# Causal mask folded into VectorE's maximum, and a new order of a pair's units, in a fused convolution, attention and spectral kernel

## The chip, the cores and the metric

One core of a Trainium2 chip runs the whole program. The metric is the device time of one execution in microseconds (us), as the median of several runs. TensorE, VectorE, ScalarE and GpSimd are called PE, DVE, ACT and POOL in the profile; SP issues most of the DMAs.

## The reference

Input `x` is 8 images of 64 channels, 32x32 pixels, float32. Three blocks follow each other, each with a residual:

```python
x = x + _L0_conv_ref(_gn(x), offset_w, offset_b, weight, bias)   # deformable 3x3 convolution
t = _to_tokens(x)                                                 # 8 x 1024 tokens x 64
t = t + _L1_attn_ref(_ln_t(t), w_q, w_k, w_v, w_o)                # 16 heads of 64, RoPE, causal
t = t + _L1_ffn_ref(_ln_t(t), sigma, phi, M_u, M_phi_plus, M_phi_minus, log_weights, gumbel)
```

What the attention computes for each image and head is

```python
att = jnp.einsum('bqhd,bkhd->bhqk', q, k) / jnp.sqrt(E)
att = jnp.where(causal, att, -jnp.inf)
att = jax.nn.softmax(att, axis=-1)
y = jnp.einsum('bhqk,bkhd->bqhd', att, v)
```

with 1024 queries and keys. The group norm `_gn` has 32 groups of two channels.

## The kernel before

The program has three stages, one after the other.

**Front.** SP loads the inputs in the order of its program. DVE takes the moments of all four pairs of images (`bn_stats`, L364), PE averages them over the channels of a group with two small matmuls (L553, L555), ACT takes the root, and DVE writes the normalised images with a border (`pad`, L390). For each pair of images PE computes the offset convolution (`conv`, L496, 9 taps x 2 halves) and then transposes the pixels (`pixels`, L509); ACT copies them out (L587), and SP writes them as a table to HBM, 16 DMAs per pair of images (`table`, L249 and L252). DVE turns the offsets into indices and weights (`draw`, L396 on). When the table of images 0 and 1 has landed and its indices are drawn, POOL gathers for the first 10 tiles of 128 tokens (L332, 9 indirect DMAs each); each tile is weighted by DVE, multiplied on PE, added to the residual and layer-normed.

**Attention.** 64 pairs of heads (8 images x 8 pairs; `NPAIR`, `NIT`). The body of the loop holds two pairs, and every engine runs the same table `SEQUENCE` of units for a pair, in order, each taking the units that are its own. The units are:

- `("rope", r)`: PE projects queries or keys of the next pair into PSUM (cost of 1024 columns), DVE multiplies by cosine and sine (L1158, L1159), POOL adds the two (`add`, L1243).
- `("upper", r)`: ACT rounds the rotated half to fp32r for the maxima (L1101).
- `("max", x)`: PE computes scores of the next pair, queries on the partitions, for the key blocks that `MAX_OF[x]` names; DVE takes the maximum over the free axis (L1149) into `mx` or `mx_half`. The causal mask of a diagonal block (key block = query block) is added on PE: four bf16 matmuls of 128 columns into the same PSUM (L920, out of `mask_b`).
- `("merge",)`: DVE merges the halves; `("row",)`: PE transposes the maxima (L964), ACT copies them negated (L1095), SP spreads them with two DMAs into `rows_m` (L865).
- `("S", u)`: PE computes the scores again, keys on the partitions, minus the maxima from `rows_m`; ACT takes the exponential (L1083). `S 0` waits for the two DMAs of `row`. POOL zeroes the diagonal blocks (`mask` in `POOL_ORDER`).
- `("value", u, lag)`: PE multiplies the probabilities by the tokens into `psY` (L1022). It needs no slot (below). With lag 1 it belongs to the pair before.
- `("leave",)`: ACT takes `psY` out (L1075). `("out", q)`: PE projects it (L1002), DVE divides by the row sums (L1128, L1131), POOL adds it to the tokens (`token`).
- `("weigh", x)`, `("fold", a)`, `("dT",)`, `("dR",)`, `("norm",)`, `("dX",)`: one tile of the deformable convolution of the next image, gathered by POOL, weighted by DVE (L1174), folded (POOL L1273, DVE L1183), multiplied on PE (L977, L984), normed by DVE (17 small dependent instructions, L1192 to L1204) and transposed by PE (L989).

The units of PE that DVE or ACT reads go round over three slots of PSUM (`SLOTS = 3`). PE may start such a unit only when the reader of the unit three places earlier is done:

```python
by = BY_ACT if UNITS[n - SLOTS][0] in BY_ACT else BY_DVE
```

So the order of the table sets how far PE can run ahead of DVE. `AHEAD` is the list for the first pair, run once ahead of the loop.

**Spectral.** Filters over the tokens of all images. The change doesn't touch it.

## Time and profile before

| | |
|---|---|
| median of 3 runs | 2934.59 us (2934.13 to 2935.37) |
| the profiled execution, its own time | 2933.56 us |
| its span | 2931.8 us |
| front, to its last copy of tokens on DVE | 0 to 199 us |
| attention, to its last projection on PE | 202 to 2260 us |
| spectral | 2268 us to the end |
| busy: PE, DVE, ACT, POOL | 94%, 75%, 45%, 59% |

The profile is of one execution. A row of the timeline gives the start, the busy time, the engine, the line of the kernel, the operation, the tile written and the tiles read. The busy time of a merged row covers several instructions, and neighbouring instructions of an engine overlap; so where it matters how long an engine is held, the text takes the distance from one start to the next.

### The profile page before, as it was taken

Reading aid. Unit: us, or ns where it says so; the run is one execution under the profiler, and the core shown is the slowest. Engines: PE = TensorE matmul, PEld = TensorE weight load, DVE = VectorE, ACT = ScalarE, POOL = GpSimd, SP = SyncE. Lnnn points to the kernel's source line nnn. Section 1 sums busy time; section 2 is a strip of 40 time slices with the busy share of each in tenths; the row PEclk is TensorE's granted clock in tenths of the full one; section 3 lists DMA queues with packets and bytes.
Section 4 is the critical chain, followed back from the end, with each engine's and each line's share of the span. In section 5 each row is a group of like instructions: output and inputs, shape, how many; then the busy total and the mean of one; then the engine's idle time right before and its main releaser. Section 6 shows DMA issues by size and latency. Waiting matters only on the chain. (4 is left out here: it accounts for less than half of the span.)

```text
span 2931.8 us, 60696 instructions
## 1 busy us (share of the span) xinstructions
PE 2741.8 (94%) x18761; PEld 1789.2 (61%) x18761; DVE 2185.6 (75%) x3909; ACT 1330.1 (45%) x1788; POOL 1740.8 (59%) x1831
## 2 busy tenths in 40 slices
PE   3639999999999999999999999999998899999998
PEld 1335655655655655656655655655655788888887
DVE  3448788788788788788888888888886675767676
ACT  1103444444444444444444444444443465656565
POOL 3746777777777777777777777777776670000000
PEclk8659999999999999999999999999999899999999
DMA  5542222222222222222222212244443553444343
GB/s 151 145 112 59 64 63 62 64 63 58 68 63 58 68 63 58 64 67 58 65 67 58 65 54 69 65 64 60 64 65 55 161 168 116 147 130 146 116 154 105
DMA packets 159644, 249.21 MB, mean 85 GB/s; under 512 B 71662, under 2 KB 93502, under 8 KB 159582
## 3 DMA queue, kind: packets, MB, share of 16 engines
q1 hardware_dynamic: 125902, 155.61, 18.8%
q0 software_dynamic: 33680, 92.71, 13.1%
q8 instruction: 46, 0.75, 0.1%
q14 instruction: 16, 0.13, 0.0%
HBM read 230.65 MB, written 17.04 MB: 84 GB/s over the span
## 5 line engine op out<-in xcount | busy, mean ns | idle before, releaser
L1083 ACT ACTIVATE attention_probs<-attention_pss 128x1024 f32<-128x1024 f32 x576 | 590.1, 1024 | 310.7 <-PE attention_pss L920 298.4
L1286 POOL DMA_INDIRECT attention_gat<-table,attention_idx x585 | 558.5, 955 | 200.0 <-issue 121.3
L920 PE MATMUL attention_pss<-attention_kq 64*128 64x512 f32 (+3 forms) x3072 | 651.8, 483 | 0.0
L1149 DVE TENSOR_REDUCE attention_mx_half<-attention_pss 128x2 f32<-128x1024 f32 (+3 forms) x520 | 513.2, 1020 | 98.5 <-PE attention_pss L920 98.5
L1022 PE MATMUL attention_psY<-attention_probs,attention_xt 128*64 128x512 f32 (+3 forms) x3120 | 574.1, 496 | 0.2 <-issue 0.2
L1642 DVE SCALAR_TENSOR_TENSOR spectral_eo<-spectral_psE,kept_sig,spectral_eo 64x512 fp32r<-64x512 f32 x512 | 384.0, 750 | 170.1 <-ACT spectral_eo L1617 163.9
L1243 POOL TENSOR_TENSOR attention_kq<-attention_tA,attention_tB 128x512 f32<-128x512 f32 x260 | 416.1, 1611 | 111.0 <-DVE attention_tB L1159 101.7
L1535 PE MATMUL spectral_psE<-spectral_tz,spectral_up 128*128 128x512 f32 (+1 forms) x2304 | 462.1, 358 | 5.8 <-DVE spectral_up L1633 5.8
L1617 ACT ACTIVATE spectral_eo<-spectral_psE,kept_sig 64x512 fp32r<-64x512 f32 x512 | 350.2, 684 | 243.9 <-PE spectral_psE L1535 238.9
L920 PE MATMUL attention_pss<-attention_rows_m,attention_ones 64*128 64x512 f32 (+2 forms) x1536 | 458.8, 530 | 0.0
L1535 PEld LDWEIGHTS spectral_psE<-spectral_tz,spectral_up 128*128 128x128 f32 x2304 | 386.5, 189 | 78.2 <-issue 6.2
L920 PE MATMUL attention_pss<-attention_nat_h 64*128 64x512 f32 (+2 forms) x1560 | 401.8, 524 | 3.1 <-DVE attention_mx_half L1149 1.9
L920 PEld LDWEIGHTS attention_pss<-attention_kq 64*128 64x128 f32 x3072 | 316.5, 186 | 48.2 <-issue 15.3
L1022 PEld LDWEIGHTS attention_psY<-attention_probs,attention_xt 128*64 128x64 f32 x3120 | 186.4, 136 | 238.4 <-issue 208.6
L1101 ACT ACTIVATE attention_nat_h<-attention_kq 128x512 fp32r<-128x512 f32 x260 | 163.9, 630 | 331.5 <-POOL attention_kq L1243 331.5
L1158 DVE TENSOR_TENSOR attention_tA<-attention_pss,attention_cosT 128x512 f32<-128x512 f32 x260 | 178.3, 686 | 164.2 <-PE attention_pss L920 163.9
L920 PE MATMUL attention_pss<-attention_xb,attention_wt 64*128 64x512 f32 x1040 | 254.9, 610 | 17.1 <-DVE attention_xT L1142 15.2
L920 PEld LDWEIGHTS attention_pss<-attention_nat_h 64*128 64x128 f32 x1560 | 168.0, 186 | 154.9 <-issue 67.4
L920 PEld LDWEIGHTS attention_pss<-attention_rows_m,attention_ones 64*128 64x128 f32 x1536 | 199.5, 186 | 95.8 <-issue 78.2
L1174 DVE TENSOR_TENSOR attention_gat<-attention_gat,conv_Wc 128x768 f32<-128x768 f32 x192 | 248.1, 1292 | 0.1
L1149 DVE TENSOR_REDUCE attention_mx<-attention_pss 128x2 f32<-128x256 f32 (+3 forms) x260 | 213.2, 821 | 13.1 <-PE attention_pss L920 13.1
L1491 POOL COPY spectral_traw<-kept_T 128x512 f32 (+1 forms) x8 | 4.7, 616 | 354.5 <-PE spectral_acc L1550 354.5
(192 smaller groups left out, 3199.0 us busy)
## 6 DMA issues: line engine op xcount, KB each, us to landing
spectral_tz<-phis SPq DMA_DIRECT2D x128, 320.5 KB, 4.6
spectral_tz<-phis SPq DMA_DIRECT2D x128, 320.0 KB, 4.2
attention_xb<-xn SPq DMA_DIRECT2D x132, 256.0 KB, 3.8
attention_gat<-table,attention_idx POOLq DMA_INDIRECT x585
table<-front_pixT SPq DMA_DIRECT2D x32, 288.0 KB
attention_wt<-in_w SPq DMA_DIRECT2D x66, 128.0 KB, 3.6
attention_xt<-xt SPq DMA_DIRECT2D x18, 128.0 KB, 2.1
attention_xs<-in_x SPq DMA_DIRECT2D x65, 32.0 KB
```

Of the source, the lines that this page charges most:

```text
L920: ins = pe.matmul(out(n), left(rows), right(rows), **flags)
L1022: ins = pe.matmul(psY[C * n:C * n + C, q:q + w], xt[:, kt, :], probs[:, u, n, at:at + w], start=(u < 2), stop=(u == NU - 1), skip_group_ch ...
L1083: act.activation(probs[:, u[1], :, :].rearrange("p n q -> p (n q)"), pss[:, slot, :], ACT.Exp, scale=float(E) ** -0.5).then_inc(s_act, 1)
L1101: act.activation(nat_h[:, r, :], kq[:, 1 - k, w, c * HB:c * HB + HB], ACT.Copy).then_inc(s_H, 1)
L1149: ins = dve.tensor_reduce(mx[:, :, i] if i < 4 else mx_half[:, :, i - 4, k0 // 4], scores, AX.X, ALU.max)
L1158: dve.tensor_tensor(tA[:, r % 2, :], pss[:, slot, 0:HB], cosT[:, cols], ALU.mult)
L1174: dve.tensor_tensor(v, v, w.unsqueeze(2).to_broadcast([P, 12, C]), ALU.mult).then_inc(s_def, 1)
L1243: pool.tensor_tensor(kq[:, 1 - k, w, c * HB:c * HB + HB], tA[:, r % 2, :], tB[:, r % 2, :], ALU.add).then_inc(s_sum, 1)
L1286: pool.indirect_dma_start(gat[:, n, :, :].rearrange("p q c -> p (q c)"), None, d.table.rearrange("r q c -> r (q c)"), bass.IndirectOffsetO ...
L1535: ins = pe.matmul(psE[:, u, :].rearrange("q (o n) -> q o n", o=2)[:, :, 2 * P - width:2 * P], up[:, x, src, a, :], both[:, :, lag:lag + wi ...
L1617: ins = act.activation(phases(k, u, rows, b), psE[rows, u, :].rearrange("q (o n) -> q o n", o=2), ACT.Copy, scale=sig[rows, k:k + 1])
L1642: ins = dve.scalar_tensor_tensor(out=phases(k, u, other, b), in0=psE[rows, u, :].rearrange("q (o n) -> q o n", o=2), scalar=sig[rows, k:k ...
```

## The change

Three things are changed.

1. **The mask.** The four mask matmuls per diagonal block are gone, and `mask_b` with its load and conversion. A float32 tile `later` of 128x512 takes its place: zeros, and the causal mask in its last 128 columns. For the eight row tiles whose last block is diagonal (widths 128, 256, 384 and 512, each twice), DVE runs a `tensor_tensor_reduce` for each of the two heads: it adds the last columns of `later` to the scores, writes the sum back to PSUM, and takes the maximum. The other four maxima stay `tensor_reduce` over both heads at once. Each unit of DVE now waits for PE with a wait of its own (`wait_apart`).
2. **The order.** `SEQUENCE`, `POOL_ORDER` and `AHEAD` have other contents. `MAX_OF` is the same.
3. **The front.** The first pair of images is loaded first and has its moments taken alone; the small weights and the other three pairs follow. The pixels of the first pair are transposed between the taps of its convolution.

```diff
-                sp.dma_start(lw[:, :], d.logw.partition_broadcast(P)).then_inc(s_small, 16)
-                sp.dma_start(gum[:, :], d.gumbel.partition_broadcast(P)).then_inc(s_small, 16)
-                sp.dma_start(sig_in[:, :], d.sigma.partition_broadcast(P)).then_inc(s_sig, 16)
-                for g in range(G):
-                    sp.dma_start(m.X[:, g, :], d.x[2 * g:2 * g + 2].rearrange("b c h w -> (b c) (h w)")).then_inc(s_x, 16)
-                sp.dma_start(pair_avg[:, :], d.pair_avg).then_inc(s_const, 16)
+                sp.dma_start(m.X[:, 0, :], d.x[0:2].rearrange("b c h w -> (b c) (h w)")).then_inc(s_x0, 16)
+                sp.dma_start(pair_avg[:, :], d.pair_avg).then_inc(s_avgw, 16)
+                sp.dma_start(m.ident[:, :], d.ident).then_inc(s_ident, 16)
                 for h in range(2):
                     sp.dma_start(offw[64 * h:64 * h + 64, :, 18 * h:18 * h + 18], d.offw).then_inc(s_offw, 16)
                     for part in range(2):
                         at_row = 64 * part + 18 * h
                         sp.dma_start(offb[at_row:at_row + 18, :], d.offb).then_inc(s_offw, 16)
+                for g in range(1, G):
+                    sp.dma_start(m.X[:, g, :], d.x[2 * g:2 * g + 2].rearrange("b c h w -> (b c) (h w)")).then_inc(s_x, 16)
+                sp.dma_start(lw[:, :], d.logw.partition_broadcast(P)).then_inc(s_small, 16)
+                sp.dma_start(gum[:, :], d.gumbel.partition_broadcast(P)).then_inc(s_small, 16)
+                sp.dma_start(sig_in[:, :], d.sigma.partition_broadcast(P)).then_inc(s_sig, 16)
...
+                def moments(first, last, count):
+
+                    for g in range(first, last):
+                        for h in range(2):
+                            ins = dve.bn_stats(gn_stats[:, g, h, :], m.X[:, g, h * HB:(h + 1) * HB])
+                    do(ins)
+                    for g in range(first, last):
+                        ins = dve.bn_aggr(gn_mv[:, g, :], gn_stats[:, g, :, :].rearrange("p a b -> p (a b)"))
+                    do(ins)
+                    do(dve.tensor_copy(dev[:, first:last], gn_mv[:, first:last, 0]))
+                    dve.sem_inc(s_mv, 1)
...
+                    dve.wait_ge(s_std, count + 1)
+                    do(dve.reciprocal(gn_rstd[:, first:last], dev[:, first:last]))
...
+                dve.wait_ge(s_x0, 16)
+                moments(0, 1, 0)
...
                 pad(0)
+                each = Chain(dve, s_weights)
+                dve.wait_ge(s_small, 32)
...
+                dve.wait_ge(s_x, 16 * (G - 1))
+                moments(1, G, 1)
                 pad(1)
+                dve.wait_ge(s_const, 32)
                 draw(0)
...
+                        if g == 0 and tap in (0, 2, 4):
+                            pixels(0, range(4 * (tap // 2), min(4 * (tap // 2) + 4, NCH)))
+                        if g == 0 and tap == 5:
+                            averages(1, 1, G)
+                        if g == 0 and tap == 8:
+                            squares(1, 1, G)
...
+                act.wait_ge(s_sq, 2)
+                act.activation(dev[:, 0:1], gn_var[:, 0:1], ACT.Sqrt).then_inc(s_std, 1)
                 act.wait_ge(s_ex, 1)
                 act.activation(soft[:, :], lw[:, :], ACT.Exp).then_inc(s_soft, 1)
+                pixels(0)
+                act.wait_ge(s_sq, 4)
+                act.activation(dev[:, 1:G], gn_var[:, 1:G], ACT.Sqrt).then_inc(s_std, 1)
+                act.wait_ge(s_offw, 96)
+                offsets(0)
+                offsets(1)
+                pixels(1)
...
-SEQUENCE = [("rope", 0), ("rope", 1), ("weigh", 0), ("upper", 0), ("rope", 2), ("upper", 1), ("value", 2, 1),
-            ("weigh", 1), ("value", 3, 1), ("value", 4, 1), ("S", 0), ("rope", 3), ("upper", 2), ("S", 1),
-            ("max", "a"), ("value", 5, 1), ("weigh", 2), ("value", 6, 1), ("max", "d"), ("max", "g"), ("upper", 3),
-            ("max", "h"), ("leave",), ("value", 7, 1), ("value", 8, 1), ("S", 2), ("fold", 1), ("S", 3),
-            ("max", "k"), ("out", 0), ("dT",), ("out", 1), ("max", "e"), ("S", 4), ("max", "i"),
-            ("value", 0, 0), ("max", "f"), ("max", "c"), ("dR",), ("norm",), ("S", 5), ("S", 6),
-            ("S", 7), ("max", "j"), ("S", 8), ("max", "b"), ("merge",), ("value", 1, 0), ("dX",),
-            ("row",)]
-POOL_ORDER = [("add", 0), ("add", 1), ("add", 2), ("mask", 0), ("add", 3), ("fold", 0), ("gather", 0),
-              ("gather", 1), ("mask", 2), ("token", 0), ("mask", 4), ("gather", 2), ("mask", 7), ("mask", 8),
+SEQUENCE = [("value", 2, 1), ("S", 0), ("weigh", 0), ("rope", 0), ("S", 1), ("rope", 1), ("rope", 2),
+            ("weigh", 1), ("S", 2), ("rope", 3), ("value", 3, 1), ("weigh", 2), ("value", 4, 1), ("max", "b"),
+            ("upper", 0), ("upper", 1), ("S", 3), ("upper", 2), ("max", "c"), ("value", 5, 1), ("value", 6, 1),
+            ("max", "e"), ("upper", 3), ("S", 4), ("max", "j"), ("fold", 1), ("value", 7, 1), ("max", "h"),
+            ("S", 5), ("leave",), ("max", "i"), ("value", 8, 1), ("max", "a"), ("max", "f"), ("dT",),
+            ("S", 6), ("max", "k"), ("max", "d"), ("value", 0, 0), ("dR",), ("max", "g"), ("S", 7),
+            ("S", 8), ("merge",), ("value", 1, 0), ("norm",), ("row",), ("out", 0), ("out", 1),
+            ("dX",)]
+POOL_ORDER = [("add", 0), ("add", 1), ("add", 2), ("add", 3), ("mask", 0), ("fold", 0), ("mask", 2),
+              ("gather", 0), ("gather", 1), ("gather", 2), ("mask", 4), ("mask", 7), ("mask", 8), ("token", 0),
               ("token", 1)]
 AHEAD = [("rope", 0), ("rope", 1), ("upper", 0), ("upper", 1), ("rope", 2), ("rope", 3), ("upper", 2),
-         ("upper", 3), ("max", "a"), ("max", "d"), ("max", "c"), ("max", "b"), ("max", "g"), ("max", "h"),
-         ("max", "e"), ("max", "f"), ("max", "k"), ("max", "i"), ("max", "j"), ("merge",), ("row",)]
+         ("upper", 3), ("max", "b"), ("max", "c"), ("max", "a"), ("max", "d"), ("max", "e"), ("max", "h"),
+         ("max", "f"), ("max", "g"), ("max", "j"), ("max", "i"), ("max", "k"), ("merge",), ("row",),
+         ("max", "a"), ("max", "b"), ("max", "c")]
...
-                            if k0 + nk == i + 1:
-
-                                for a in range(2):
-                                    ins = both(lambda n: out[:, n * HB + first - P:n * HB + first],
-                                               lambda rows: mask_b[rows, 1 + a, :], lambda rows: mask_b[rows, 3 + a, :],
-                                               start=False, stop=True, skip_group_check=True)
...
-                    dve.wait_ge(s_full, n + 1)
+                    wait_apart(dve, s_full, n + 1, s_apart)
                     if u[0] == "max":
                         first = 0
                         for i, k0, nk in MAX_OF[u[1]]:
                             scores = pss[:, slot, :].rearrange("p (n c) -> p n c", n=2)[:, :, first:first + nk * P]
-                            ins = dve.tensor_reduce(mx[:, :, i] if i < 4 else mx_half[:, :, i - 4, k0 // 4], scores, AX.X, ALU.max)
+                            top = mx[:, :, i] if i < 4 else mx_half[:, :, i - 4, k0 // 4]
+                            if k0 + nk == i + 1:
+                                for n in range(2):
+                                    ins = dve.tensor_tensor_reduce(scores[:, n, :], scores[:, n, :], later[:, HB - nk * P:HB], 1.0,
+                                                                   LOWEST, ALU.add, ALU.max, top[:, n:n + 1])
+                            else:
+                                ins = dve.tensor_reduce(top, scores, AX.X, ALU.max)
...
+    later = np.zeros((P, HB), f)
+    later[:, HB - P:] = np.where(p[None, :] > p[:, None], MASKED, 0)
```

The mask and the order, as the instructions stand. PE, the end of a pair in the loop, before (`mask_b` are the mask matmuls, `rows_m` with `kq` the S units, `attention_xn` is `dX`, `attention_mx` is `row`, `xb` is a rope):

```order
L920 MATMUL attention_pss<-attention_nat_h 128x256 x2
L920 MATMUL attention_pss<-attention_mask_b 128x128 x4
L1022 MATMUL attention_psY<-attention_probs,attention_xt 64x512 x2
L1057 REGISTER_ALU
L78 REGISTER_ALU
L989 MATMUL attention_pss<-kept_ident,attention_xn 64x128
L1055 REGISTER_ALU
L963 REGISTER_ALU
L964 MATMUL attention_pss<-kept_ident,attention_mx 16x128
L1057 REGISTER_ALU
L969 ISA
L920 MATMUL attention_pss<-attention_xb,attention_wt 128x512 x2
```

and after the change:

```order
L984 MATMUL attention_pss<-kept_ident,attention_mx 16x128
L1075 REGISTER_ALU
L1022 ISA
L1022 MATMUL attention_pss<-attention_wo,attention_yT 128x130 x4
L1075 REGISTER_ALU
L1022 MATMUL attention_pss<-attention_wo,attention_yT 128x130 x4
L1075 REGISTER_ALU
L78 REGISTER_ALU
L1009 MATMUL attention_pss<-kept_ident,attention_xn 64x128
L1030 REGISTER_ALU
L1042 MATMUL attention_psY<-attention_probs,attention_xt 64x128 x2
L1042 MATMUL attention_psY<-attention_probs,attention_xt 64x384 x2
```

Here `row` stands ahead of the two projections (`wo`) and `dX`, and behind one value the next instructions are `S 0` (before, three ropes and three values stood between `row` and `S 0`).

DVE, the maxima `f` and `k` of a pair after the change; before, each was one `TENSOR_REDUCE`:

```order
L1175 TENSOR_REDUCE attention_mx_half<-attention_pss 128x2
L78 REGISTER_ALU
L1172 ISA attention_pss,attention_mx_half<-attention_pss,attention_later 128x512
L1172 ISA attention_mx_half 128x1
L1172 ISA attention_pss,attention_mx_half<-attention_pss,attention_later 128x512
L1172 ISA attention_mx_half 128x1
```

One maximum over both heads has become four instructions: per head the sum with maximum, and one that writes out the maximum and reads no tile.

## Rows read from the trace of the kernel before

**Rows 1.** Windows: stretch and length; busy of PE, PEld, DVE, ACT, POOL; clock; DMA.
```profile
250.00:2250.00 2000.00, 1984.57 (x14468) 1181.41 (x14464) 1611.00 (x2867) 927.00 (x1177) 1483.89 (x1528) 1.00 0.26 63
```
**Rows 2.** Timeline of PE around one pair.
```profile
999.69 0.50 PE L920 MATMUL attention_pss<-attention_rows_m,attention_ones 64*128 64x512 f32 x2
...
1002.95 0.29 PE L920 MATMUL attention_pss<-attention_mask_b 64*128 64x128 bf16 x4
1003.16 1.94 PE L1022 MATMUL attention_psY<-attention_probs,attention_xt 128*64 128x512 f32 x8
1005.03 0.49 PE L920 MATMUL attention_pss<-attention_nat_h 64*128 64x512 f32 x2
...
1010.57 0.29 PE L920 MATMUL attention_pss<-attention_mask_b 64*128 64x128 bf16 x4
1010.86 1.15 PE L1002 MATMUL attention_pss<-attention_wo,attention_yT 128*128 x8
...
1018.96 0.79 PE L920 MATMUL attention_pss<-attention_rows_m,attention_ones 64*128 64x512 f32 x1
...
1020.04 0.79 PE L920 MATMUL attention_pss<-attention_rows_m,attention_ones 64*128 64x512 f32 x1
...
1025.13 0.28 PE L964 MATMUL attention_pss<-kept_ident,attention_mx 128*16 128x128 f32 x1
1025.33 2.85 PE L920 MATMUL attention_pss<-attention_xb,attention_wt 64*128 64x512 f32 x12
1028.11 2.81 PE L1022 MATMUL attention_psY<-attention_probs,attention_xt 128*64 128x128 f32 x20
1030.84 0.50 PE L920 MATMUL attention_pss<-attention_rows_m,attention_ones 64*128 64x512 f32 x2
```
**Rows 3.** Groups by line and form: count | busy us, mean ns | idle before.
```profile
L1149 DVE TENSOR_REDUCE attention_mx_half<-attention_pss 128x2 f32<-128x1024 f32 x325 | 390.7, 1220 | 98.5 <-PE attention_pss L920 98.5
...
L920 PE MATMUL attention_pss<-attention_mask_b 64*128 64x128 bf16 x2080 | 174.1, 222 | 0.0
...
L1149 DVE TENSOR_REDUCE attention_mx_half<-attention_pss 128x2 f32<-128x512 f32 x65 | 44.3, 682 | 0.0
```
**Rows 4.** Timeline of DVE in the same pair.
```profile
1027.21 0.68 DVE L1159 TENSOR_TENSOR attention_tB<-attention_pss,attention_sinT 128x512 f32<-128x512 f32 x1
1027.80 0.68 DVE L1158 TENSOR_TENSOR attention_tA<-attention_pss,attention_cosT 128x512 f32<-128x512 f32 x1
...
1038.02 2.35 DVE L1149 TENSOR_REDUCE attention_mx_half<-attention_pss 128x2 f32<-128x1024 f32 x2
...
1050.96 0.15 DVE L1195 TENSOR_SCALAR attention_var<-attention_mv 128x1 f32<-128x1 f32 x1
1051.15 0.15 DVE L1198 TENSOR_SCALAR attention_rstd<-attention_var 128x1 int32<-128x1 int32 x1
```
**Rows 5.** Timeline of DVE at the start of the program.
```profile
1.48 0.06 DVE L217 MEMSET front_offb<- 128x1 f32 x1
1.49 0.11 DVE L218 MEMSET front_zrow<- 35x64 f32 x1
...
13.94 4.84 DVE L364 BATCH_NORM_STATS2 front_gn_stats<-early_X 128x6 f32<-128x512 f32 x8 [1.72 <-DMA early_X<-in_x]
```
**Rows 6.** Timeline of SP's DMA queue, the maxima's spreading.
```profile
1025.80 1.48 SPq L865 DMA_DIRECT2D attention_rows_m<-attention_rows_b  x2
```
**Rows 7.** DMA issues: line, engine, count, KB each, median us to landing.
```profile
early_X<-in_x SPq DMA_DIRECT2D x4, 512.0 KB, 6.2
...
xn<-attention_xT SPq DMA_DIRECT2D x64, 32.0 KB, 1.9
```
**Rows 8.** Timeline of PE: the first convolution.
```profile
23.33 9.65 PE L496 MATMUL front_psO<-front_xpad,front_offw 128*64 128x512 f32 x36 [1.61 <-DVE front_xpad L390]
```
**Rows 9.** Timeline of ACT: the last pixels of the first pair of images.
```profile
36.13 0.42 ACT L587 ACTIVATE front_pixT<-front_psP 128x128 f32<-128x128 f32 x2 [0.53 <-PE front_psP L509]
```
**Rows 10.** Timeline of POOL: ahead of the first gather.
```profile
49.45 0.19 POOL L329 COPY front_idx<-conv_IDX 128x9 int32<-128x9 int32 x1 [22.79 <-DMA table<-front_pixT]
```

124 lines of the change are left out of this document (50 added, 74 removed).

## The prediction

> **What bounds the kernel now.** I read the windows first. In 2000 us inside the attention PE is busy 1984.6 us at a granted clock of 1.00 (2.4 GHz), DVE 1611.0, POOL 1483.9 and ACT 927.0 [rows 1]. The attention holds 64 pairs, so a microsecond per pair is 64 us. The timeline of PE gives the length of a pair: from one S 0 to the next, 999.69 to 1030.84, is 31.15 us [rows 2]. Of that DVE is busy 1611.0 / 2000 x 31.15 = 25.1 us [rows 1]. So PE sets the time, DVE is the next in line with 6 us of idle per pair, and POOL has 8. The reader should see in [rows 2] that PE goes from unit to unit with hardly a hole. The wait of DVE's big maxima for PE, 98.5 us over 325 of them [rows 3], says the same from the other side: DVE waits for PE.
>
> The front is another matter. Its rows form a chain: moments of all images (13.94), first convolution (23.33), last pixels (36.5), table landed and first gather (49.45) [rows 5, 8, 9, 10]. What follows, 10 tiles behind POOL's gathers, starts with the last of these.
>
> **The mask on PE.** 2080 matmuls are taken out, 32 for each of 65 computations of the maxima. From the first of a group of four to what follows is 1002.95 to 1003.16, 0.21 us, and 1010.57 to 1010.86, 0.29 us [rows 2]. Eight groups at 0.21 are 1.7 us per pair. The upper bound is their whole busy time, 174.1 / 65 = 2.7 us [rows 3]; the lower bound is nothing, if they only fill time in which PE would wait for a slot. I take 1.7, since PE shows no such waits. PE alone would then make a pair of 31.15 - 1.7 = 29.45 us. A part of this is still small waits for DVE and ACT. Unit by unit, with an S at 1.08 us (1018.96 to 1020.04), a rope at 0.93 (three from 1025.33 to 1028.11) and a value at 0.91 (three from 1028.11 to 1030.84) [rows 2], I get 28.6 us for PE's own work without the mask; that is an estimate.
>
> **The mask on DVE.** Eight reductions per pair become 16 sums with maximum and 16 small writes of the result. Nothing in the trace shows the new instruction, so I bound it by the nearest rows.
> - The sum with maximum. Two TENSOR_TENSORs of 512 with one operand in PSUM start 0.59 us apart though each lasts 0.68 [rows 4]. A reduction of 1024 lasts 1220 ns and one of 512 lasts 682 ns [rows 3], so 512 elements cost 0.54 us and the rest is fixed; as two reductions of 1024 take 2.35 us together [rows 4], they start 1.13 us apart, of which about 0.06 is fixed. The elements stay the same (5120 per pair). Only the fixed part is paid 16 times instead of 8: 8 x 0.06 = 0.5 us.
> - The write of the result. It has no input, and the nearest row is a MEMSET of one column: 0.06 us long, the next one starting 0.01 us behind it [rows 5]. The other end is a small dependent instruction: the next starts 0.19 us later (1050.96 to 1051.15) [rows 4]. So 16 writes cost 0.2 to 3.0 us; I take 0.06 each, 1.0 us, because nothing waits for the result before the next head's sum.
>
> DVE's own work grows from 25.1 to 25.1 + 0.5 + 1.0 = 26.6 us per pair, below PE's 28.6.
>
> Here the Trainium skill speaks against the change. "VectorE: DVE Perf Modes", section "The DRAIN you can't avoid", says that after every VectorE instruction the pipeline drains before the next starts, so the number of instructions counts. The trace doesn't agree for neighbours of one kind: 0.59 us from start to start against 0.68 of duration [rows 4]. Its neighbouring section, "Two Vector instructions with no wait between them", counts an accumulator's output as a second instruction, which the listing above shows, and has it start without a hold when the output's partitions stay the same; no row here shows that one.
>
> **The order.** DVE is now within 2 us of PE, and PE may run ahead by three slots only, so the order decides how much of 26.6 us of work can be put into a pair of 28.6 us. I laid the new table out with the durations above, PE's units against DVE's, and looked for idle time of DVE that nothing fills:
> - rope 1 stands behind S 1 on PE: 1.08 + 0.93 us of PE against 1.2 us for a rope on DVE leave 0.7;
> - dT, S 6 and k stand behind f. S 6 takes the slot that f leaves, so k comes 1.08 us plus its own 0.3 and 0.2 for the handing over after f is read: 1.6;
> - short waits at rope 0, e and g, about 0.3 each: 0.9;
> - norm's 17 steps wait for each other, 0.04 us each (0.15 of 0.19 is busy) [rows 4]: 0.7.
>
> That gives 26.6 + 0.7 + 1.6 + 0.9 + 0.7 = **30.5 us per pair**, with PE and DVE bound together round the loop. DVE's work from rope 0 to the end of norm, and behind it PE's dX, closes the ring. The old order hid such waits under 6 us of slack. The gain is (31.15 - 30.5) x 64 = 42 us.
>
> The single values between other units cost about as much as in a row (0.91) [rows 2]. POOL has its adds, masks and gathers in another order; with 23.1 us of work (1483.9 / 2000 x 31.15) [rows 1] it keeps 7 us of slack, and I cost that at nothing. If this cover were gone, the weighting on DVE, which waits for the gathers, would be the first to be late.
>
> **The front.** X of the first pair is now the first DMA, and its moments are 2 of the 8 statistics that took 4.84 us [rows 5]. The DMA lands 6.2 us after its issue [rows 7], at about 10 us. With 1.2 us for the statistics and the old 4.5 us from there to the pad, less 0.3 for fewer groups, the convolution starts at about 15.5 instead of 23.3 [rows 8]. Its pixels are out when five of nine taps are through, 6.5 us later, at 22 instead of 36.5 [rows 9]; the table follows by the same 12.9 us as before (36.55 to 49.45) [rows 9, 10] and is there at 35. The indices need the whole convolution, 9.65 us with 2.2 of pixels in it [rows 8], the copy, four transposes and about 4 us of drawing: 34. Both meet at 35 against 49.45. I take **14 us** (8 if offw lands late or the small weights, which DVE now does behind the first pad, hold it up; 16 at best). Taking the first pair's maxima has three more maxima at its end, and S 0 of the loop now stands near the front, behind the DMAs of row: 2 us lost, once. Moving lw, gum and sigma behind X costs nothing: POOL's scaling of mixu with them is long done when the gathers start.
>
> **The sum.** 2933.6 (the profiled execution, 1.0 below the median of the runs) - 42 - 14 + 2 = 2880, and 1.0 more for the median: **2881 us**.
>
> **The rivals.**
> - *PE stays the bound.* If the waits in my list overlap with each other, or the weighting is cheaper where it now stands, PE goes at 29.2 us. For it: PE's busy 1984.6 of 2000 [rows 1] and 26.6 us of DVE. Against it: a ring of three slots, with DVE at 91%. Time: 2881 - 1.3 x 64 = 2798.
> - *S 0 waits for the maxima.* Now the spreading has a slack of 5.7 us (1025.13 to 1030.84) [rows 2]. It takes 0.67 us to SP's issue, then 1.48 for two issues [rows 6] and a landing of up to 1.9 us [rows 7]: 3.3 to 4.1 us. In the new order two projections, dX and one value lie between row and S 0, 1.0 + 1.0 + 0.2 + 0.9 and row's own 0.2 = 3.3. From 3.4 us on it decides; at 4.1 it costs 0.7 us per pair, 45 us: 2926. A change that does nothing in the attention (the mask's matmuls hidden, 2923) looks the same.
> - *The new instructions don't overlap*, and it becomes slower. The place is the unit of a diagonal maximum on DVE. If each sum pays its full duration, 0.085 us more, it is 16 x 0.085 = 1.4 us per pair, 31.9 us and 2881 + 90 = 2971. If each write pays 0.19 as a dependent instruction does [rows 4], it is 16 x 0.13 = 2.1 us, 32.6 us and 3015. It decides from 0.65 us per pair, or 0.04 us per new pair of instructions. By the skill's rule on the drain, named above, the first of these holds.
>
> **How the numbers follow.** A measurement of this kernel can tell about 0.2%, or 6 us, from no change. My forecast has 0.36, PE as the bound 0.20, the wait of S 0 or no effect 0.15, the slow case 0.29. Of the third 0.09 is faster, 0.05 the same and 0.01 slower; of the first 0.01 and of the last 0.02 are the same. Faster is then 0.35 + 0.20 + 0.09 = 0.64, the same 0.08, slower 0.28. The range reaches from 2795, where PE bounds it, to 2985, beyond the sums at full duration; the dear writes and a still faster PE are left out. Within the forecast's own case it is 2850 to 2910.
>
> **What would show it.** In the profile after: no `mask_b`; the first gather at about 35 us; sums of 512 at 0.68 to 0.70 us starting 0.66 us apart with their write between them; DVE busy 26.6 of 30.5 us; PE below 96% in the attention, with its waits ending on DVE, most at S 6 and dX. A write of 0.15 us or more makes it the slow case; PE at 99% makes it the fast one; a wait at S 0 for rows_m the third. A first gather later than 42 us makes the front's part wrong.

## The result and the profile after

The changed kernel takes **3023.34 us** (3018.50 to 3024.63, 4 runs), against 2934.98 us of the kernel before (2934.13 to 2938.47, 4 runs) in the same comparison. The ratio is 1.0297, interval 1.0280 to 1.0313: 88 us slower, where 2881 us was forecast. One execution of the run with real indices, below, fell into a slow state (4477.4 us at a granted clock of 0.55) and is left out of its time.

| | before | after |
|---|---|---|
| profiled execution, its span | 2931.8 us | 3021.8 us |
| busy: PE, DVE, ACT, POOL | 94%, 75%, 45%, 59% | 91%, 75%, 43%, 58% |
| first gather | 49.45 us | 37.08 us |
| mean length of the 64 pairs, from `row` to `row` | 31.46 us | 32.95 us |

The last line of the table is from the first and the last `row` on PE. Timeline of PE, before:

```profile
236.75 0.37 PE L964 MATMUL attention_pss<-kept_ident,attention_mx 128*16 128x128 f32 x1 [1.74 <-DVE attention_mx L1167]
...
2250.44 0.28 PE L964 MATMUL attention_pss<-kept_ident,attention_mx 128*16 128x128 f32 x1
```

and after, with one of the last ten pairs between them:

```profile
225.21 0.37 PE L984 MATMUL attention_pss<-kept_ident,attention_mx 128*16 128x128 f32 x1 [3.10 <-DVE attention_mx L1193]
...
2033.70 0.28 PE L984 MATMUL attention_pss<-kept_ident,attention_mx 128*16 128x128 f32 x1
2071.01 0.28 PE L984 MATMUL attention_pss<-kept_ident,attention_mx 128*16 128x128 f32 x1
...
2333.76 0.28 PE L984 MATMUL attention_pss<-kept_ident,attention_mx 128*16 128x128 f32 x1
```

The attention is 95 us longer (2108.5 against 2013.7 us between these rows), its start 11.5 us earlier, and what follows its last `row` 6.7 us longer. The 95 us come in two stretches, 34 us in the first and 60 us in the second. The first 54 pairs alternate between 31.59 and 32.52 us (before: 31.15 and 31.62). The last ten take 37.2 to 37.8 us each, as 2033.70 to 2071.01 shows; before, they were like the others.

The windows answer to [rows 1] (same columns). After:

```profile
250.00:1250.00 1000.00, 956.29 (x6081) 499.25 (x6077) 830.08 (x2149) 439.63 (x577) 738.29 (x749) 1.00 0.23 62
...
2050.00:2250.00 200.00, 176.98 (x1055) 90.69 (x1052) 144.23 (x376) 77.52 (x101) 127.86 (x128) 0.91 0.39 53
```

DVE is busy 830.1 of 1000 us, 26.6 us per pair, as forecast. PE's share has fallen from 99.2% to 95.6%; "below 96%" was forecast too. What was not forecast is how long a pair takes with it: 32.1 us and not 30.5 up to the 54th, and 37.5 in the last ten. In the last stretch the granted clock is 0.91 and the DMA engines are busy 39% of the time while moving less.

The sums on DVE answer to [rows 3, 4]. Timeline of DVE after, at the end of a pair:

```profile
989.76 0.73 DVE L1172 CUSTOM_DVE_ANT_0 attention_pss<-attention_pss,attention_later 128x512 f32<-128x512 f32 x1
990.41 0.14 DVE L1172 DVE_READ_ACCUMULATOR2_ANT attention_mx_half<- 128x1 f32 x1
990.41 0.73 DVE L1172 CUSTOM_DVE_ANT_0 attention_pss<-attention_pss,attention_later 128x512 f32<-128x512 f32 x1
991.06 0.14 DVE L1172 DVE_READ_ACCUMULATOR2_ANT attention_mx<- 128x1 f32 x1
991.06 0.73 DVE L1172 CUSTOM_DVE_ANT_0 attention_pss<-attention_pss,attention_later 128x512 f32<-128x512 f32 x1
```

A sum of 512 with its write takes 0.65 us from start to start; 0.66 was forecast. The write lasts 0.14 us, but the next sum starts with it.

### The profile page after: what moved, and what is told of

It reads as the page before. It is cut to its first block and busy times, and to the rows that moved or that the text cites. A ratio compares the mean times of both kernels' runs of the same rounds, so it can differ in the third digit from the quotient of the medians.

```text
span 3021.8 us, 59245 instructions
## 1 busy us (share of the span) xinstructions
PE 2738.3 (91%) x16691; PEld 1641.3 (54%) x16691; DVE 2276.5 (75%) x5487; ACT 1305.0 (43%) x1790; POOL 1761.7 (58%) x1831
## 3 DMA queue, kind: packets, MB, share of 16 engines
q0 software_dynamic: 33680, 92.71, 13.4%
## 5 line engine op out<-in xcount | busy, mean ns | idle before, releaser
L946 PE MATMUL attention_pss<-attention_kq 64*128 64x512 f32 (+3 forms) x3072 | 626.5, 489 | 0.0
L1042 PE MATMUL attention_psY<-attention_probs,attention_xt 128*64 128x512 f32 (+3 forms) x3120 | 603.3, 501 | 13.9 <-POOL attention_probs L1288 13.9
L1172 DVE CUSTOM_DVE_ANT_0 attention_pss<-attention_pss,attention_later 128x512 f32<-128x512 f32 (+3 forms) x1046 | 484.1, 521 | 80.6 <-PE attention_pss L946 80.6
L946 PE MATMUL attention_pss<-attention_rows_m,attention_ones 64*128 64x512 f32 (+2 forms) x1536 | 390.6, 507 | 42.4 <-DMA attention_rows_m<-attention_rows_b 36.2
L1175 DVE TENSOR_REDUCE attention_mx_half<-attention_pss 128x2 f32<-128x1024 f32 x260 | 318.1, 1225 | 97.5 <-PE attention_pss L946 97.5
L946 PE MATMUL attention_pss<-attention_nat_h 64*128 64x512 f32 (+2 forms) x1566 | 382.4, 507 | 3.6 <-DVE attention_mx L1172 2.2
L946 PEld LDWEIGHTS attention_pss<-attention_kq 64*128 64x128 f32 x3072 | 277.5, 189 | 69.8 <-issue 45.5
L1280 POOL TENSOR_TENSOR kept_T<-kept_T,attention_scaled 128x256 f32 x260 | 219.7, 845 | 136.9 <-DVE attention_scaled L1151 96.1
L946 PEld LDWEIGHTS attention_pss<-attention_rows_m,attention_ones 64*128 64x128 f32 x1536 | 148.6, 189 | 156.4 <-DMA attention_rows_m<-attention_rows_b 68.2
L1200 DVE TENSOR_TENSOR attention_gat<-attention_gat,conv_Wc 128x768 f32<-128x768 f32 x192 | 198.7, 1035 | 3.7 <-issue 2.5
```

The costliest lines, as they stand in the source:

```text
L946: ins = pe.matmul(out(n), left(rows), right(rows), **flags)
L1042: ins = pe.matmul(psY[C * n:C * n + C, q:q + w], xt[:, kt, :], probs[:, u, n, at:at + w], start=(u < 2), stop=(u == NU - 1), skip_group_ch ...
L1172: ins = dve.tensor_tensor_reduce(scores[:, n, :], scores[:, n, :], later[:, HB - nk * P:HB], 1.0, LOWEST, ALU.add, ALU.max, top[:, n:n + 1])
L1175: ins = dve.tensor_reduce(top, scores, AX.X, ALU.max)
L1200: dve.tensor_tensor(v, v, w.unsqueeze(2).to_broadcast([P, 12, C]), ALU.mult).then_inc(s_def, 1)
L1280: pool.tensor_tensor(t, t, scaled[:, quarter, n, :, :].rearrange("p t c -> p (t c)"), ALU.add).then_inc(s_T, 1)
```

## The experiments

Each comparison had its own runs of the kernel before, 2934.8 to 2936.9 us. The pair's length is the mean of the 64 distances from `row` to `row` on PE.

| run | us | ratio to before (95%) | pair |
|---|---|---|---|
| front alone | 2926.2 | 0.9968 (0.9957 to 0.9980) | 31.47 |
| mask alone | 2970.0 | 1.0120 (1.0103 to 1.0136) | 31.95 |
| order alone | 3045.9 | 1.0369 (1.0352 to 1.0387) | 33.14 |
| front and mask | 2947.7 | 1.0045 (1.0028 to 1.0062) | 31.84 |
| no mask in the maxima | 2902.3 | 0.9884 (0.9867 to 0.9900) | 30.90 |
| changed, values ahead of S 0 | 3076.4 | 1.0479 (1.0461 to 1.0496) | 33.75 |
| changed, real indices | 2969.3 | 1.0120 (1.0100 to 1.0141) | 32.11 |
| changed, early table load | 3002.6 | 1.0227 (1.0210 to 1.0244) | 32.62 |
| front, no mask | 2888.1 | 0.9837 (0.9820 to 0.9853) | 30.90 |
| mended (both mends) | 2941.3 | 1.0022 (1.0012 to 1.0031) | 31.70 |
| mended, no mask | 2924.2 | 0.9964 (0.9949 to 0.9978) | 31.36 |
| mask alone, direct waits | 2963.2 | 1.0092 (1.0075 to 1.0109) | 31.88 |
| mended, masks first | 2919.2 | 0.9940 (0.9926 to 0.9953) | 31.34 |
| front, no mask, both mends | 2887.7 | 0.9832 (0.9819 to 0.9846) | 30.90 |

### One part of the change at a time

The edits are the hunks of the diff, put on the kernel before. Front alone:

> The kernel before with the front's part of the change alone (first pair of images loaded first, its moments alone, its pixels between the taps); mask and order as before. Both theories: the first gather starts 12.4 us earlier as in the profile after (37.08 against 49.45), and nothing else moves: 2935 - 12 = 2923 us, pairs at 31.15 and 31.62 as before.

Mask alone:

> The kernel before with the mask's part alone (mask matmuls out, sums with maximum on DVE, a wait of its own for each of DVE's units); front and order as before. Theory A (the new order is what costs): PE is relieved and DVE still has slack under the old order, so a pair is 0.8 to 1.7 us shorter, 2935 - 51 to - 109 = 2826 to 2884 us. Theory B (the sums on DVE are what costs: with them DVE sets the ring's pace in any order): a pair is 0.3 to 0.8 us longer, 2955 to 2985 us. Both: the last ten pairs are like the others, since row stands three ropes and three values ahead of S 0.

Order alone:

> The kernel before with the new order alone (SEQUENCE, POOL_ORDER, AHEAD); mask on PE and front as before. Theory A (order costs): the pairs up to the 54th take what they take after, about 32.1 us, plus 0 to 1.7 us for the mask matmuls, and the last ten again some 5.6 us more each: 3035 to 3120 us. Theory B (DVE's sums cost): the first 54 pairs are at 31.4 us as before, only the last ten are longer: 2935 + 40 to + 56 = 2975 to 2991 us. If the last ten pairs are not longer than the others, the stall at S 0 needs the shorter lead of PE over DVE, and neither theory has it right.

Front and mask, order as before:

> The changed kernel with SEQUENCE, POOL_ORDER and AHEAD as before (front and mask new, order old). Theory A: 12 us below the run with the mask alone, 2814 to 2872 us. Theory B: 2943 to 2973 us.

The front gains 10 us and leaves the pairs alone, as both theories had it. The mask costs 34 us and the order 110 us, so A and B are each half right. The parts don't add up (-10 + 34 + 110 would be 134 us, and the whole costs 88): on top of front and mask the order costs 77 us. Its last ten pairs cost 5.8 us each there and 6.1 with the mask on PE, its other 54 cost 0.24 and 0.85 us.

The mask's pairs are 31.41 and 31.99 us (+0.3 to +0.4), and six of them take some 2 us more. In these six the granted clock stands at 0.50 (1.2 GHz) for some 3 us, within the first 6 us behind `row`; in the others it is 1.00, but for the very first pair, which is at 0.90 to 0.95 in all kernels. An ordinary pair and a long one, by windows:

```profile
430.90:462.90 32.00, 30.37 (x196) 17.16 (x196) 26.57 (x70) 15.28 (x19) 23.42 (x25) 1.00 0.22 61
494.30:528.40 34.10, 32.01 (x195) 17.69 (x196) 26.55 (x70) 15.18 (x19) 23.35 (x25) 0.95 0.23 65
```

PE's waits shown further down stand just before it. Why the clock falls in six pairs and not in the others, no run shows.

The order has the last ten pairs at 37 to 38 us with the mask on PE too, so that stall needs no earlier DVE: of the three parts it belongs to the order alone.

Where the mask's cost lies is seen at the end of a pair. Timeline of PE with the mask alone:

```profile
1006.75 0.27 PE L980 MATMUL attention_pss<-kept_ident,attention_xn 128*64 128x128 f32 x1 [0.48 <-DVE attention_mx_half L1143]
1007.54 0.28 PE L955 MATMUL attention_pss<-kept_ident,attention_mx 128*16 128x128 f32 x1 [0.51 <-DVE attention_mx L1164]
1008.66 2.85 PE L917 MATMUL attention_pss<-attention_xb,attention_wt 64*128 64x512 f32 x12 [0.84 <-DVE attention_xT L1133]
```

In the old order `dX`, `row` and the first rope each wait for DVE, which comes late out of its longer maxima. Before, PE went through these places without a hole in one pair of two [rows 2].

### What the mask costs on PE by itself

```diff
-                            if k0 + nk == i + 1:
-
-                                for a in range(2):
-                                    ins = both(lambda n: out[:, n * HB + first - P:n * HB + first],
...
```

> The kernel before with the mask matmuls taken out and nothing put in their place: the maxima are taken over masked keys too, DVE keeps its eleven reductions. It shows what the mask on PE costs by itself. Theory P (my prediction: PE's busy time is work, and each mask group costs what it lasts): a pair is 1.7 us shorter, 2935 - 109 = 2826 us. Theory R (PE's busy time of 99% holds waits for slots: a rope takes 0.46 us where its slot is free and 0.86 to 0.96 elsewhere, an S 0.69 against 1.09; DVE and PE are bound together round the ring): the time given up by the mask is filled with longer waits, a pair is 0 to 0.6 us shorter, 2895 to 2935 us.

The pairs fall from 31.15 and 31.62 to 30.56 and 31.06: 0.56 us, a third of the 1.7 us at which I had priced the matmuls. R's number holds, at its upper edge; its reason doesn't, as the rows below show. Against this run the sums on DVE cost 31.95 - 30.90 = 1.05 us per pair, 68 us. The windows of the two (no mask, then mask alone) say how much work that is:

```profile
250.00:2150.00 1900.00, 1862.46 (x12020) 1075.29 (x12016) 1557.73 (x2771) 896.12 (x1140) 1435.46 (x1478) 1.00 0.26 64
```

```profile
250.00:2150.00 1900.00, 1819.27 (x11617) 1022.41 (x11617) 1581.71 (x4104) 869.27 (x1100) 1385.12 (x1427) 0.99 0.25 62
```

DVE works 1557.73 / 1900 x 30.90 = 25.3 and 1581.71 / 1900 x 31.95 = 26.6 us per pair. So 1.3 us more on DVE cost 1.05 us.

How much of a pair PE needs for itself is seen in its timeline after the change, where a rope and an S find their slots free:

```profile
1001.32 1.02 PE L946 MATMUL attention_pss<-attention_xb,attention_wt 64*128 64x512 f32 x4
1001.78 0.80 PE L946 MATMUL attention_pss<-attention_rows_m,attention_ones 64*128 64x512 f32 x2
1002.42 1.02 PE L946 MATMUL attention_pss<-attention_kq 64*128 64x512 f32 x4
...
1010.01 0.39 PE L946 MATMUL attention_pss<-attention_rows_m,attention_ones 64*128 64x512 f32 x2
1010.24 1.02 PE L946 MATMUL attention_pss<-attention_kq 64*128 64x512 f32 x4
1010.70 0.74 PE L946 MATMUL attention_pss<-attention_nat_h 64*128 64x384 f32 x2
```

Theory R took the rope for 0.46 us (1001.32 to 1001.78), an S for 0.69 (1010.01 to 1010.70), and the rest of PE's busy time for waits. The rows say otherwise. A record outlasts the turn of its matmul by 0.16 us: at 1010.01 it is 0.39 us long, and the next matmul starts 0.23 us later. At 1001.78 the same two matmuls last 0.80 us, and the next starts 0.64 us later: they stand 0.41 us behind the rope, the second half of which still runs. So the rope takes 1002.42 - 1001.32 - 0.23 = 0.87 us, and the S takes 0.23 + 1.02 - 0.16 = 1.09. The prediction's 0.93 and 1.08 were near: PE's busy time is mostly work.

With these 0.16 us taken off each record, the time of PE splits in three. This is an estimate from all its records between the third and the 53rd `row`, in us per pair. A change is one between matmuls on 64 or 65 rows and on 128 (the first number of the form, as in `64*128`). A gap of 0.09 us stands at 650 of the 750 changes of the kernel before, 50 have none and 50 a longer one; of 10600 neighbours on the same rows 10500 have no gap. Waits are what the longer gaps have above 0.09.

| run | pair | work | gaps of 0.09 | waits |
|---|---|---|---|---|
| before | 31.43 | 29.65 | 1.46 | 0.32 |
| no mask in the maxima | 30.87 | 28.57 | 1.52 | 0.77 |
| mask alone | 31.93 | 28.81 | 1.52 | 1.59 |
| order alone | 32.30 | 29.78 | 1.71 | 0.81 |
| changed | 32.11 | 28.69 | 1.72 | 1.71 |
| mended, masks first | 31.35 | 28.64 | 1.67 | 1.03 |

In the kernel before, PE needs 31.1 of 31.4 us for itself, so it did set the time. The mask was 1.1 us of its work and not 1.7: of the 0.21 us read at 1002.95 in [rows 2], 0.09 are the gap at the change behind it, which stays. Of the 1.1 us, 0.45 came back as waits, most of them at `row` for DVE's maxima. With the sums on DVE the waits are 1.59 us, 0.6 each at `dX` and at `row`; that the work is 28.81 instead of 28.57 comes mostly from the pairs at the lower clock. In the changed kernel PE needs 30.4 us for itself, so the forecast of 30.5 left it almost nothing for waits.

### The last ten pairs

Gathers run one tile ahead, 10 tiles on (`FIRST`); the last ten gather tiles behind the 64th, whose indices are a memset of 0. First their results are left unused but their rows made real:

```diff
                         ins = dve.tensor_copy(m.IDX[:, first:first + NT, :], idxf[:, :, b, :])
+                        if g == G - 1:
+                            ins = dve.tensor_copy(m.IDX[:, B * NT + 6 * b:B * NT + 6 * b + 6, :], idxf[:, 0:6, b, :])
```

> The changed kernel with real indices instead of zeros for the gathers of the tiles behind the last one (copied from other tiles; their results are not used). Nothing else changes. Theory A (128 times the same row makes a gather slow, and its packets hold up the DMA of the maxima): the last ten pairs fall from 37.5 to 32.1 us like the others, 3023 - 54 = 2969 us. Rival (the landing is late in the last pairs for a reason that has nothing to do with the indices): no change, 3023 us.

The last ten pairs are at 31.6 and 32.5 us like the others, and 54 us are gone. Theory A holds, its time too (2969). Whether it is the repeating of a row or that row itself that makes the gathers slow, this run can't tell. The same 200 us by windows, in the kernel before early and late, then with real indices in the changed one:

```profile
1000.00:1200.00 200.00, 198.81 (x1445) 116.93 (x1442) 161.25 (x281) 94.37 (x119) 147.04 (x151) 1.00 0.23 63
2050.00:2250.00 200.00, 198.78 (x1463) 119.86 (x1461) 161.36 (x295) 93.01 (x119) 149.51 (x156) 1.00 0.43 63
```

```profile
2050.00:2250.00 200.00, 191.76 (x1220) 100.07 (x1218) 164.91 (x431) 88.52 (x117) 147.94 (x151) 1.00 0.24 66
```

The slow gathers were there before the change: 63 GB/s cost a DMA share of 0.43 instead of 0.23. Nothing waited for them. What the new order adds is the wait of S 0, here after the change (PE, then SP's queue):

```profile
2108.73 0.28 PE L984 MATMUL attention_pss<-kept_ident,attention_mx 128*16 128x128 f32 x1
...
2116.70 0.80 PE L946 MATMUL attention_pss<-attention_rows_m,attention_ones 64*128 64x512 f32 x2 [3.56 <-DMA attention_rows_m<-attention_rows_b]
2117.29 1.91 PE L946 MATMUL attention_pss<-attention_kq 64*128 64x512 f32 x4
2118.99 1.92 PE L946 MATMUL attention_pss<-attention_xb,attention_wt 64*128 64x512 f32 x4
```

```profile
2109.41 1.46 SPq L891 DMA_DIRECT2D attention_rows_m<-attention_rows_b  x2
```

The maxima land some 5.8 us after their issue is over (2109.41 + 1.46 to 2116.70). PE waits 3.56 us, and behind the wait the same matmuls last 1.91 us instead of 1.02: the granted clock fell (0.91 over the window) after PE had stood still. With real indices S 0 starts 4.2 to 4.4 us behind `row`, here 7.97. So of the 5.4 us that each of the last ten pairs takes more, 3.5 come ahead of S 0, and the other 1.9 behind it, at the lower clock.

More distance between `row` and S 0, for the same stall:

```diff
-SEQUENCE = [("value", 2, 1), ("S", 0), ("weigh", 0), ("rope", 0), ("S", 1), ("rope", 1), ("rope", 2),
-            ("weigh", 1), ("S", 2), ("rope", 3), ("value", 3, 1), ("weigh", 2), ("value", 4, 1), ("max", "b"),
+SEQUENCE = [("value", 2, 1), ("value", 3, 1), ("value", 4, 1), ("S", 0), ("weigh", 0), ("rope", 0), ("S", 1), ("rope", 1), ("rope", 2),
+            ("weigh", 1), ("S", 2), ("rope", 3), ("weigh", 2), ("max", "b"),
```

> The changed kernel with values 3 and 4 of the pair before moved ahead of S 0, so that 5.2 us of PE's work instead of 3.3 lies between row and S 0. Theory A (the last ten pairs are long since the maxima's DMA lands late): the last ten fall from 37.5 to 32.5 to 35.5 us, the others stay within 0.5 us; 3023 - 20 to - 55, so 2968 to 3003 us. Rival (the last ten are long for another reason, such as a late gather or late loads): they stay at 37.5, and the time stays within 10 us of 3023.

The stall shrinks (the last ten are 34.6 to 36.9 us at a granted clock of 1.00 or 0.95, and one is 38.6 at 0.91), but the kernel becomes 53 us slower: the other pairs grow by 1.1 to 1.4 us, where I had allowed 0.5. The timeline of PE tells what the two values had covered:

```profile
1007.31 1.02 PE L946 MATMUL attention_pss<-attention_xb,attention_wt 64*128 64x512 f32 x4
1009.81 0.39 PE L946 MATMUL attention_pss<-attention_nat_h 64*128 64x256 f32 x2 [1.48 <-ACT attention_nat_h L1121]
```

The first maximum needs the last rope through DVE, POOL and ACT. A value that stands between other units is worth the wait that it fills, not its own 0.9 us.

### The table load at the head of the body

```diff
                 with act.Fori(0, NIT) as it:
+                    act.activation(warm[0:1, 0:1], m.ident[0:1, 0:1], ACT.Exp)
```

> The changed kernel with one small exponential of ACT that waits for nothing, put at the head of the loop's body: ACT's table load then runs ahead of S 0 instead of between S 0's scores and its exponential. Theory T (the load of 1.28 us, once per two pairs, lies on the path since the new order makes S 0 the first unit of ACT in the body): the pairs of 32.5 us fall to 31.6, 32 of them, 3023 - 29 = 2994 us. Rival (the pair at the head of the body is longer through the branch of the loop on PE and DVE, as the 0.5 us of before): no change, 3023 us.

Timeline of ACT in the changed kernel, at the head of the body:

```profile
1001.60 1.28 ACT L1103 ACT_TABLE_LOAD   x1 [5.66 <-PE attention_pss L946]
1002.90 1.94 ACT L1103 ACTIVATE attention_probs<-attention_pss 128x1024 f32<-128x1024 f32 x2
```

and with the early exponential:

```profile
987.11 1.28 ACT L1132 ACT_TABLE_LOAD   x1
988.41 0.20 ACT L1132 ACTIVATE attention_warm<-kept_ident 1x1 f32<-1x1 f32 x1
992.71 1.02 ACT L1104 ACTIVATE attention_probs<-attention_pss 128x1024 f32<-128x1024 f32 x1 [4.10 <-PE attention_pss L947]
```

Before, it stood here:

```profile
993.78 1.28 ACT L1101 ACT_TABLE_LOAD   x1
998.13 0.63 ACT L1101 ACTIVATE attention_nat_h<-attention_kq 128x512 fp32r<-128x512 f32 x1 [3.06 <-POOL attention_kq L1243]
```

The load goes with ACT's first activation in the body. Before, this was an `upper`, whose single wait came behind the load; so the load was over 3.06 us early. Now it is S 0's exponential, which waits twice in the code, for its scores and for the value that last read its `probs`; the load starts when the scores are there, and rope 1 on PE waits for the exponential. The pairs of 32.52 fall to 31.74 us and 21 us are gone: theory T, with 0.8 instead of 0.9 us for each of 27 loads. The last ten pairs keep their length (37.4 us), since there S 0 waits for the maxima anyway. The Trainium skill says in "ScalarE activation tables: per-element evaluation and per-set limits", section "Table sets in the compiler and the runtime", that the compiler places the loads per block. The trace agrees, with 32 loads for 32 bodies in either kernel.

### Both mends, and what the sums cost in the new order

> The changed kernel with both mends: real indices for the tiles behind the last one, and the early small exponential. If the two losses are apart: 3023 - 51 - 20 = 2952 us, with pairs of 31.6 and 31.7 us to the end. That would be within 0.3% of front and mask under the old order (2948 us), so that the new order would be worth nothing and cost nothing beside those two. If they overlap, 2960 to 2972.

> The same as the mended one, with the sums with maximum replaced by plain reductions over both heads (maxima over masked keys too), each DVE unit's wait still apart: it shows what the sums cost in the new order. Theory R (DVE is the later of the two round the ring): as in the old order, where they cost 1.05 us per pair (2970 against 2902), the pair falls from 31.65 to 30.6: 2952 - 67 = 2885 us. Rival (in the new order the waits at the head of a pair decide, not DVE's work): 2935 to 2952 us.

The two losses are apart and more than add up (82 us together, 54 and 21 singly): with real indices the early load is worth its 0.8 us in the last five bodies too, 4 us of the 7. The time is 2941.3 us, 11 below the expectation and 6 below front and mask under the old order. That the new order gains these 6 us is not shown: both kernels' ordinary pairs have a mean of 31.66 us (31.60 and 31.71 here, 31.41 and 31.90 there), and the old order has four pairs at the lower clock, 2 us each.

Without the sums the pair goes from 31.70 to 31.36, so they cost 0.34 us here and not 1.05. The time, 2924.2 us, lies between theory R (2885) and the rival (2935 to 2952), nearer to the rival: PE needs 30.2 us for itself here, and its waits fall only from 1.40 to 1.18 us.

Direct waits for all units of DVE that don't begin with a sum, on the mask alone:

> The mask in DVE under the old order and front (2970 us before), with the wait apart kept only for the maxima that begin with a sum; the others wait directly again. Theory W (each wait apart holds DVE's queue by some 0.05 us and lies on the path at 12 units of a pair): 0.3 to 0.6 us per pair less, 2932 to 2951 us. Rival (it is hidden in DVE's waits for PE; the sums alone cost the 1.05 us): 2970 us.

It gives 5 to 7 us (7 from time to time, 5 with each run against its own kernel before), between the two and little above the noise. The sums themselves carry most of the cost.

### The last step of norm

POOL's masks, on the mended kernel:

```diff
-              ("gather", 0), ("gather", 1), ("gather", 2), ("mask", 4), ("mask", 7), ("mask", 8), ("token", 0),
+              ("gather", 0), ("gather", 1), ("mask", 4), ("mask", 7), ("mask", 8), ("gather", 2), ("token", 0),
```

> The mended kernel (2941 us) with POOL's masks 4, 7 and 8 ahead of the last three gathers instead of behind them. After the change norm's last step on DVE takes 0.83 to 0.88 us instead of 0.31 and the copy behind it 0.46 instead of 0.19, and in the trace POOL's masks 7 and 8 run just then. Theory C (an affine select on POOL slows the DVE operation that runs beside it): with the masks moved away from it that step falls to about 0.35 us; PE waits for it at dX, 0.66 us per pair, so up to 0.5 us per pair less: 2941 - 10 to - 32 = 2909 to 2931 us, unless the masks, now waiting for S 8, push gathers and tokens onto the path. Rival (the step is slow for what its operands are, not for its neighbour): the step stays at 0.83 us, 2941 us or more.

DVE and POOL in the changed kernel, by their timelines:

```profile
997.05 0.89 DVE L1230 TENSOR_SCALAR attention_xn<-kept_T,attention_mv,attention_rstd 128x64 f32 x1
998.06 0.47 DVE L1232 COPY attention_xt_new<-attention_xn 128x63 f32<-128x63 f32 x1
```

```profile
996.89 0.65 POOL L1288 TENSOR_SCALAR_AFFINE_SELECT attention_probs<-attention_probs 128x512 f32<-128x512 f32 x1
997.48 0.41 POOL L1291 TENSOR_SCALAR_AFFINE_SELECT attention_probs<-attention_probs 128x256 f32<-128x256 f32 x1
997.84 0.63 POOL L1288 TENSOR_SCALAR_AFFINE_SELECT attention_probs<-attention_probs 128x512 f32<-128x512 f32 x1
```

and DVE with the masks first, where gathers run beside norm's end:

```profile
981.62 0.37 DVE L1234 TENSOR_SCALAR attention_xn<-kept_T,attention_mv,attention_rstd 128x64 f32 x1
982.11 0.20 DVE L1236 COPY attention_xt_new<-attention_xn 128x63 f32<-128x63 f32 x1
```

By groups over 300 to 1900 us (busy us, mean ns), the mended kernel and the one with the masks first:

```profile
L1234 DVE TENSOR_SCALAR attention_xn<-kept_T,attention_mv,attention_rstd 128x64 f32 x50 | 41.4, 829 | 1.8
```

```profile
L1234 DVE TENSOR_SCALAR attention_xn<-kept_T,attention_mv,attention_rstd 128x64 f32 x51 | 17.2, 337 | 1.8
```

The step falls from a mean of 829 to 337 ns, the pair from 31.70 to 31.34 and the kernel to 2919.2 us, 22 us less. Theory C holds. The Trainium skill's page "SBUF — State Buffer", section "SBUF: two separate sides", says that GpSimd and some VectorE operations share one port pair, under a lock that is held for a whole instruction; with it the step would wait for the end of the select it meets. The trace agrees for the step: it starts at 997.05, the select ends at 996.89 + 0.65 = 997.54, and 0.37 us more make 997.91, against its end at 997.94. For the copy it doesn't: the last select ends at 998.47, and the copy, 0.20 us long without a neighbour, is over at 998.53. Spans on POOL are rough, and which port the two used no run here shows.

### A version that beats both, and a control

> The kernel before with the front's part of the change and the mask matmuls taken out (maxima over masked keys too; order as before). If the gains of the two parts add up: 2935 - 10 - 34 = 2891 us, below both kernels. If the front's gain is lost again somewhere once the pairs are shorter: 2902.

> The fastest kernel so far (front new, no mask in the maxima, order as before, 2888 us) with both mends of the changed kernel. If the late landing and the table load cost only where the new order lays them onto the path, nothing changes: 2888 us within 0.2%. If they cost in the old order too, 2 to 20 us less.

Front without a mask in the maxima is 2888.1 us, 46.8 us below the kernel before: the gains add up (3 us better than their sum). The maxima are there taken over masked keys too. The softmax divides by its own sum, so a larger subtrahend cancels out, as long as no masked score stands so far above the allowed ones that their exponentials vanish. With the mask kept, the fastest is the one with the masks first, 2919.2 us. The control is at 2887.7 us, so both mends are worth nothing in the old order: it had neither loss on its path.

## Why the prediction was wrong

- **"28.6 us for PE's own work"** failed, and with it the room that the forecast gave to PE's waits. The prices per unit were near, but the sum lacks the gaps of 0.09 us at changes of rows: PE needs 30.4 us for itself in the new order, and PE as the bound at 29.2 us was never to be had. The mask was priced at 1.7 us and was 1.1. "So PE sets the time" was right for the kernel before, to 0.3 us.
- **The pair before** was read as 31.15 us from one pair; the mean is 31.46, since the pair at the head of the body takes 31.62. A view of one pair of a body of two missed 20 us of the attention, and hid the place where the table load matters.
- **DVE's own work, 26.6 us**, was right, and 0.65 us per sum with its write. That its growth by 1.5 us would fit under PE was wrong; it cost 1.05 us in the old order, since DVE hands over later at `dX` and `row`, where PE waits.
- **"The list of idle time, 30.5 us"** is the step that failed. The list held only waits of DVE for PE. The pairs took 32.11 us: 30.4 of PE's own and 1.7 of waits, at `dX` for norm's last step 0.73, at rope 1 behind the table load 0.31, at the value behind `dX` 0.26, at dT 0.23 and at S 0 0.15 us. Not in it were the table load (0.8 us per two pairs, 21 us) and the neighbour on POOL (0.36 us per pair, 22 us, though I had costed "POOL's order at nothing"). With both mends and the masks first the pair is 31.34 us, with 1.0 us of waits: S 0 0.29, the value behind `dX` 0.26, `dX` 0.24, dT 0.22. What these would take to go no run tested. Of the two waits of PE that the forecast named, the one at `dX` came and the one at S 6 did not.
- **"S 0 waits for the maxima"** was a rival at 0.15 with the right place and the wrong size; the forecast itself put nothing there. I took a landing of at most 1.9 us from [rows 7]; in most pairs that holds and S 0 waits 0.3 us at most, but behind the gathers with zeros as indices it was 5.8 us. The ten pairs with it cost 54 us. The median landing of another DMA is no bound for the worst time of this one.
- **"The new instructions don't overlap"** was the rival on the slower side, at 0.29. The sign came out, the mechanism didn't: a sum starts 0.65 us after the one before and lasts 0.73. The rule of the Trainium skill in "VectorE: DVE Perf Modes", "The DRAIN you can't avoid", would have each start behind the end of the last; the trace does not show that.
- **The front, 14 us**, measured 12.4 at the first gather and 10 to 12 in the time. Within its bounds.

Together: 3023.3 - 82 (both mends) - 22 (POOL) = 2919 us, 38 above the forecast. These are 0.84 x 64 = 54 us of pairs at 31.34 instead of 30.5, less the 20 us by which the mean pair of before was taken too low, and 4 us of the front and the end.

## What to carry to other kernels

Take an engine's own need from its records before pricing what a change takes off it: the distance between starts in a row of like matmuls, plus the gaps that stand at every change of kind. What the period has above it are the waits, and no order can win more than these. The distance to the next unit's first record is not a unit's length, since that record can begin while the unit still runs; a record that is longer than elsewhere says so. Work handed from an engine near its bound to one with slack can cost time wherever the second hands over to the first. When units are reordered, look at what becomes the first instruction of a loop's body on each engine, at what runs on POOL beside DVE's dependent steps, and at the worst landing, not the median one, of each DMA that now has less time. Give padding gathers spread indices.

## What the runs showed of the hardware

- A gather in which all 128 indices are the row 0 is dear: over the whole program the gathers' queue has the same packets and bytes with zeros and with real indices, but a share of 13.4% against 10.6% of the engines' time. The pages of DMA queues, changed kernel and then with real indices:

```profile
q0 software_dynamic: 33680, 92.71, 13.4%
```

```profile
q0 software_dynamic: 33680, 92.71, 10.6%
```

  That is 404.9 - 314.6 = 90 us of all 16 engines for 90 gathers, 1.0 us each, and another queue's 4 KB landed 3 to 4 us later behind them.
- The write of an accumulator lasts 0.14 us, and the next sum starts with it. Sum and write of 512 columns take 0.65 us from start to start, 0.59 us a TENSOR_TENSOR of 512 without a write [rows 4].
- A matmul's record outlasts its turn on PE by 0.16 us (0.39 against 0.23 from start to start), and a gap of 0.09 us stands at 650 of 750 changes between 64 or 65 rows and 128.
- The first activation of a loop's body brings a table load of 1.28 us every time round; where that activation has two waits in the code, the load ran behind the first of them here, and the activation follows 1.30 us after the load's start.
- An fp32 step of 64 columns on DVE takes 0.83 to 0.89 us beside affine selects of POOL and 0.31 to 0.37 us beside gathers.
